# Reordering layer norms, value tiles and operand halves in a one-core gated cross-attention kernel

## The reference

```
x = x + tanh(g_xattn[0]) * L0_xattn(layernorm(x), ctx)        # 16 heads x 64, keys/values from 77 context tokens
x = x + tanh(g_ffn[0])   * L0_ffn(layernorm(x))               # ternary weights, int8-like activations, silu(gate)*up
x = x + tanh(g_xattn[1]) * L1_xattn(layernorm(x), ctx)
x = x + tanh(g_ffn[1])   * L1_ffn(layernorm(x))               # one expert's gelu ffn times its router probability

def L1_xattn(xx, ee):
    x = ln(xx, ln1)
    x = x + mha(x, x, a1, causal=True)      # 16 heads x 32, 512 keys; softmax over all keys, then the causal mask
    x = ln(x, ln2)
    return x + mha(x, ee, a2, causal=False) # keys and values from the 77 context tokens
# mha: xn = ln(x, lnx); yn = ln(y, lny); q, k, v; softmax(q k / sqrt(d)); o @ li1 + b + x;
#      then x_out + gelu(ln3(x_out) @ li2 + b) @ li3 + b
```

## Time and profile before

| | |
|---|---|
| median of 3 runs | 386.19 us (384.49 to 387.12) |
| the profiled execution | 386.85 us, span 385.1 us |
| mean granted TensorE clock in it | 0.972 |
| busy | PE 330.1 (86% of the span), DVE 285.7, ACT 271.5, POOL 122.7 us |

### The profile page before, as it was taken

The page is one execution under the profiler, slowest core; times in us unless marked ns, Lnnn a source line. Parts: engine busy times, 40 slices in busy tenths (PEclk is TensorE's granted clock), DMA queues, the critical chain, the costliest instruction groups (busy, mean ns, idle before and its releaser), DMA issues.

```text
span 385.1 us, 6932 instructions
## 1 busy us (share of the span) xinstructions
PE 330.1 (86%) x2165; PEld 233.5 (61%) x2165; DVE 285.7 (74%) x736; ACT 271.5 (70%) x957; POOL 122.7 (32%) x227
## 2 busy tenths in 40 slices
PE   5989999717698888898999889899896999978993
PEld 4868887503334554555646555576674888765673
DVE  0767779597886995979979889855586887846515
ACT  2378897847364998989999899914248888754441
POOL 1317665236512332223233233311023533421200
PEclk9999999968898999999999999999998999999999
DMA  6900000000019869403970896000000000000001
GB/s 197 361 9 1 2 3 0 0 1 3 0 43 211 184 143 211 84 2 69 212 159 1 178 212 214 3 2 0 2 2 1 1 2 0 3 0 2 0 2 54
DMA packets 6908, 24.75 MB, mean 64 GB/s; under 512 B 1451, under 2 KB 1528, under 8 KB 6136
## 3 DMA queue, kind: packets, MB, share of 16 engines
q1 hardware_dynamic: 6872, 24.31, 26.3%
HBM read 7.00 MB, written 0.52 MB: 20 GB/s over the span
## 4 chain that ended last, share of the span: by engine, by line
PE 45%; DVE 23%; ACT 16%; DMA 5%; issue 5%; SPq 3%; POOL 1%; DVEq 0%; ACTq 0%
PE ps L444 7%; PE ps L568 7%; PE ps L546 7%; ACT pring L1247 6%; PE ps L626 5%; PE ps L608 5%; DVE nm L1647 4%; PE ps L475 3%; SPq L884 3%; ACT arena L1121 3%; PE ps L496 3%; DMA stack<-sides 3%; PE ps L702 2%; ACT arena L1231 2%; PE ps L738 2%
## 5 line engine op out<-in xcount | busy, mean ns | idle before, releaser
L1647 DVE TENSOR_REDUCE nm<-ps 128x1 f32<-128x512 f32 x128 | 81.2, 678 | 17.0 <-PE ps L702 17.0
L1247 ACT ACTIVATE pring<-ps,nm 128x512 f32<-128x512 f32 x128 | 89.0, 725 | 6.4 <-DVE nm L1647 6.4
L1121 ACT ACTIVATE arena<-ps,nmx 128x77 f32<-128x77 f32 x256 | 79.2, 344 | 14.4 <-DVE nmx L1417 14.1
L1009 POOL TENSOR_SCALAR_AFFINE_SELECT pring<-pring 128x128 f32<-128x128 f32 x128 | 37.4, 295 | 80.9 <-ACT pring L1247 80.9
L702 PE MATMUL ps<-stack 128*128 128x512 f32 x128 | 55.2, 491 | 5.8 <-ACT pring L1247 2.4
L1121 ACT ACTIVATION_READ_ACCUMULATOR arena<-ps,nmx 128x1 f32 x256 | 57.2, 223 | 0.0
L974 POOL TENSOR_TENSOR arena<-arena,rden 128x616 f32<-128x616 f32 x32 | 39.2, 1226 | 51.3 <-DVE rden L1426 51.3
L444 PE MATMUL ps<-ident,pring 128*128 128x128 f32 x320 | 46.9, 275 | 5.9 <-ACT arena L1231 4.3
L444 PEld LDWEIGHTS ps<-ident,pring 128*128 128x128 f32 x320 | 36.5, 140 | 19.8 <-POOL pring L1009 10.7
L568 PEld LDWEIGHTS ps<-arena 128*128 128x128 f32 x320 | 38.9, 191 | 13.1 <-DVE arena L1433 11.7
L568 PE MATMUL ps<-arena 128*128 128x128 f32 x320 | 42.5, 280 | 4.9 <-DVE arena L1433 4.9
(11 more groups left out here) (149 smaller groups left out, 525.9 us busy)
## 6 DMA issues: line engine op xcount, KB each, us to landing
stack<-sides SPq DMA_DIRECT2D x32, 256.0 KB, 5.0
stack<-arena SPq DMA_DIRECT2D x16, 256.0 KB, 5.1
stack<-hid SPq DMA_DIRECT2D x12, 256.0 KB, 5.0
wa_sb<-in_wa SPq DMA_DIRECT2D x1, 1536.0 KB, 14.1
early<-in_w SPq DMA_DIRECT2D x2, 512.0 KB, 8.0
stack<-hid SPq DMA_DIRECT2D x8, 128.0 KB, 2.5
arena<-in_wa SPq DMA_DIRECT2D x1, 1024.0 KB, 4.8
pring<-in_wf SPq DMA_DIRECT2D x1, 768.0 KB, 10.7
```

The costliest lines, as they stand in the source:

```text
L1009: pool.affine_select(out=blk, in_=blk, compare_op=ALU.is_gt, fill=0.0, base=0, pattern=[[1, P]], channel_multiplier=-1).then_inc(masked, 1)
L1121: ins = act.activation(Pc[:, i % PC_SLOTS, h * HS:h * HS + M], bank(where[key])[:, h % 4 * HS:h % 4 * HS + M], ACT.Exp, bias=nmx[:, i % 4, ...
L1247: release(act.activation(pring[:, n % 2, i, :], bank(f"S{i}"), ACT.Exp, bias=nm1[:, n % 8, i:i + 1], accum_out=den1[:, n % 8, i:i + 1]), ( ...
L1647: dve.tensor_reduce(nm1[:, n % 8, i:i + 1], bank(f"S{i}"), AX.X, ALU.max, negate=True).then_inc(nm1_ready, 1)
```

## The change

1. Lead-in of the causal attention. VectorE does `low_half` 0 to 3 and the copies of value tiles 1 and 3 first and only then `ln1_gain(1)` and `ln1_bias(1)`. TensorE makes all four value tiles of batch 0 before the first scores (banks T0, T1, S1, S3) instead of two before and two in n = 0; the unread matmuls behind them are six into S0 instead of ten into S3. ScalarE copies tile 2 before the loop.
2. Causal attention, n = 5 and 6 on ScalarE. The "k" evacuation of batch 1 moves from n = 6 (between the exponentials) to the end of n = 5, and `sums_across(0)` from the end of n = 5 to n = 6, between the exponentials.
3. Second cross attention. `ln2_gain(1)` moves ahead of the units; `ln2_bias(1)` from i = 2, 3 to i = 0, 1; `ln_stats("a2", 1)` from i = 4 to two halves in i = 2 and 3; `ln_norm("a2", 1)` from i = 5 to two halves in i = 4 and 5; GpSimd's `power` from j = 3 to j = 2. The two additions of `a2_li1_b` move from i = 7, 8 to i = 10, 11. TensorE gets unread matmuls into bank A, five at i = 1 and two at i = 2.
4. Tails of both cross attentions. `ln_stats` of "a2f" and "f0", batch 0, from i = 13 to two halves in i = 13 and 14; `ln_norm` from i = 14 to 15; `power` from j = 12 to 13. `scale_x(0)` stays in i = 15, now behind `ln_norm`. The third ternary matrix is written at i = 17 instead of 13; `gate_up(0)` waits for two matrices and the first down product for the third.

```diff
-            def keep_busy(count):
-
+            def keep_busy(count, res="S3"):
+
+                pe.wait_ge(*last[res])
                 for _ in range(count):
-                    pe.matmul(bank("S3"), identb[:, :], wf0b[:, 0, :], start=True, stop=True)
+                    pe.matmul(bank(res), identb[:, :], wf0b[:, 0, :], start=True, stop=True)
...
+                    if site == "a2" and i in (1, 2):
+                        keep_busy(5 if i == 1 else 2, "A")
...
                         xq_transposes(0)
-                        pe.wait_ge(wq_ready, 3)
+                        pe.wait_ge(wq_ready, 2)
                         gate_up(0)
...
                     if t == 0:
+                        pe.wait_ge(wq_ready, 3)
                         claim(pe, res, ("out", "f0", b), filled_by=(f0_done, j + NT))
...
-            for t in range(2):
-                project_values(t, f"T{t % 2}")
-            keep_busy(10)
+            for t, res in enumerate(("T0", "T1", "S1", "S3")):
+                project_values(t, res)
+            keep_busy(6, "S0")
...
-                if n == 0:
-                    project_values(2, "T0")
                 if n < NHB:
                     scores(n, 2)
                     scores(n, 3)
-                if n == 0:
-                    project_values(3, "T1")
...
-                    if site == "l0" and j == 12:
+                    if site == "l0" and j == 13:
                         power("f0", batches=[0])
-                    if site == "a2" and j == 3:
+                    if site == "a2" and j == 2:
                         power("a2", batches=[1])
-                    if site == "a2" and j == 12:
+                    if site == "a2" and j == 13:
                         power("a2f", batches=[0])
...
             copy_values(0)
+            copy_values(2)
...
-                    if u == 0 and n in (5, 6):
-                        a1_evac(1, "qk"[n - 5])
-                if n == 0:
-                    copy_values(2)
-                if n >= HG and n % HG == 1:
+                    if u == 0 and n == 5:
+                        a1_evac(1, "q")
+                    if u == 0 and n == 6:
+                        sums_across(0)
+                if n == 5:
+                    a1_evac(1, "k")
+                if n > HG + 1 and n % HG == 1:
                     sums_across(n // HG - 1)
...
-                    if site == "a2" and i == 13:
-                        ln_stats("a2f", 0, xo)
-                    if site == "a2" and i == 14:
+                    if site == "a2" and i in (13, 14):
+                        ln_stats("a2f", 0, xo, range(2 * i - 26, 2 * i - 24))
+                    if site == "a2" and i == 15:
                         ln_norm("a2f", 0, xo)
...
-                    if site == "l0" and i == 13:
-                        ln_stats("f0", 0, r)
-                    if site == "l0" and i == 14:
+                    if site == "l0" and i in (13, 14):
+                        ln_stats("f0", 0, r, range(2 * i - 26, 2 * i - 24))
+                    if site == "l0" and i == 15:
                         ln_norm("f0", 0, r)
-                    if site == "l0" and i == 15:
                         scale_x(0)
                     if site == "a2" and i in (0, 1):
-                        ln2_gain(1, range(2 * i, 2 * i + 2))
+                        ln2_bias(1, range(2 * i, 2 * i + 2))
                     if site == "a2" and i in (2, 3):
-                        ln2_bias(1, range(2 * i - 4, 2 * i - 2))
-                    if site == "a2" and i == 4:
-                        ln_stats("a2", 1, x1)
-                    if site == "a2" and i == 5:
-                        ln_norm("a2", 1, x1)
-                    if site == "a2" and i in (7, 8):
-                        did(dve.tensor_tensor(xb[:, i - 7, :, :], x1[:, i - 7, :, :], row4("a2_li1_b"), ALU.add))
+                        ln_stats("a2", 1, x1, range(2 * i - 4, 2 * i - 2))
+                    if site == "a2" and i in (4, 5):
+                        ln_norm("a2", 1, x1, tiles=range(2 * i - 8, 2 * i - 6))
+                    if site == "a2" and i in (10, 11):
+                        did(dve.tensor_tensor(xb[:, i - 10, :, :], x1[:, i - 10, :, :], row4("a2_li1_b"), ALU.add))
...
-                    if site == "l0" and i in (9, 11, 13):
-                        ternary_bf16(i // 2 - 4)
+                    if site == "l0" and i in (9, 11, 17):
+                        ternary_bf16((9, 11, 17).index(i))
...
-            ln1_gain(1)
-            low_half(0)
-            ln1_bias(1)
-            for m in range(1, 4):
+            for m in range(4):
                 low_half(m)
             copy_values(1)
+            copy_values(3)
+            ln1_gain(1)
+            ln1_bias(1)
...
                 if n == 0:
-                    copy_values(3)
                     ln_stats("a1", 1, x1)
...
             ln_stats("ln2", 1, xo)
+            ln2_gain(1)
             cross("a2")
```

More of the change, by code:

```diff
@@ L668, in _ @@
                 if n == NB * NT:
-                    pe.wait_ge(*last["S3"])
                     keep_busy(6)
@@ L1307, in settle, with ln_stats @@
                     dve.wait_ge(*freed.pop(0))
-            def ln_stats(site, b, src):
-                for t in range(NT):
+            def ln_stats(site, b, src, tiles=range(NT)):
+                for t in tiles:
                     did(dve.bn_stats(stats[:, b, t, :], src[:, b, t, :]))
                 settle()
-                for t in range(NT):
+                for t in tiles:
                     did(dve.bn_aggr(mv[:, b, t, :], stats[:, b, t, :]))
+                if tiles[-1] < NT - 1:
+                    return
                 settle()
@@ L1320, in ln_stats, with ln_norm @@
                     .then_inc(var_ready, 1)
-            def ln_norm(site, b, src, affine=None, dst=None):
+            def ln_norm(site, b, src, affine=None, dst=None, tiles=range(NT)):
                 dve.wait_ge(rstd_ready, nth(site, b))
                 if affine is None:
-                    for t in range(NT):
+                    for t in tiles:
                         ins = dve.tensor_scalar(xn[:, b, t, :], src[:, b, t, :], mv[:, b, t, 0:1],
                                                 rstd[:, b, t:t + 1], ALU.subtract, ALU.mult)
+                    if tiles[-1] < NT - 1:
+                        did(ins)
+                        return
+                    settle()
                 else:
```

## The result

The changed kernel took 384.99 us (median of 20 executions, 382.45 to 386.07) against 387.63 (median of 20, 384.49 to 388.84) for the kernel before: ratio 0.9926, 95% interval 0.9905 to 0.9947. That is 2.64 us in the medians, 0.7%, faster than before and less than forecast. The median of before shown ahead of the prediction, 386.19, was of three of these executions.

A forecast was written before the change was run, and what follows sets the result against it. No engine was taken to bound the whole; TensorE, busiest, works 86% of the span. 2.05 - 0.65 + 2.0 + 1.1 + 0.35 = 4.85 us off 386.85 gave 382.0, or 381.4 against the 386.19 median; own range 380.2 to 382.6, wider 379.6 to 384.6.

The forecast's parts named there:

- lead-in (c): Causal attention's lead-in: head 1's first maxima follow head 0's without a gap, 2.05 us gained, bounds 0.5 to 2.6.
- exchange (d, e): Causal attention, n = 5 and 6: value product waits for the sums, delaying projection 8 and head 7's scores, 0.65 us lost.
- units of the second attention (f): Second cross attention: full clock held by unread matmuls, norm in halves, unit 8's scores earlier; 2.0 us gained, bounds 0.7 to 2.4.
- second tail (g, h): Second cross attention's tail: half the stats leave i = 13, unit 15's maxima start earlier; 1.1 us gained, bounds 0.6 to 1.3.
- first tail (a): First cross attention's tail: the same, but `scale_x` waits behind the norm; 0.35 us gained, bounds 0 to 0.7.
- fourth rival: At n = 6 TensorE idles 1.6 us and falls to half clock, costing at most 1.75 us: 383.1, chance 0.10.
- third rival: Lead-in bound by stacks: head 2's stack slips 1 to 1.5 us, reordering gives 0.8 us: 382.7, chance 0.12.

The follow-up runs named there:

- e10: The kernel before, no edit, one more single profiled execution: 384.90 us.
- e11: The kernel before, no edit, another single profiled execution: 386.37 us.
- e14: The kernel before, no edit, a single profiled execution to catch a long one: 386.32 us.
- e15: The kernel before, no edit, another single profiled execution to catch a long one: 388.20 us.
- e8: The changed kernel measured and profiled again, no edit: 385.64 us, ratio 0.9945; its profiled execution took 382.55 us.
- e12: The changed kernel, no edit, a single profiled execution: 383.94 us.
- e16: The changed kernel, no edit, a single profiled execution to catch a long one: 383.00 us.
- e18: The changed kernel, no edit, a single profiled execution to catch a long one: 384.80 us.
- e17: The changed kernel, no edit, a single profiled execution: 385.05 us.
- e4: The changed kernel with the exchange undone (k evacuation back in head 6, sums back at the end of head 5): 382.24 us, ratio 0.9891.
- e5: The changed kernel plus six unread matmuls into bank B at n = 6, ahead of the waiting value product: 382.89 us, ratio 0.9883.
- e6: The kernel before with 18 instead of 10 unread matmuls ahead of the causal attention's first scores: 385.41 us, ratio 0.9961.
- e2: The kernel before with only the second cross attention's changes, including its seven unread matmuls: 385.19 us, ratio 0.997.
- e1: The kernel before with only the lead-in changes (halves, four value tiles, copies, six unread matmuls): 384.73 us, ratio 0.9959.
- e13: The kernel before, nothing reordered, with 18 instead of 10 lead-in unread matmuls and seven in the second cross attention: 384.97 us, ratio 0.9955.
- e9: The changed kernel with the sums, then the k evacuation directly behind them, at the end of head 5: 382.76 us, ratio 0.9889.

## Why the prediction was wrong

The mechanisms of the sum were all seen; most of its terms were mis-sized, and one choice between rivals was wrong. In the means over the profiled executions (five of before: this study's first, e10, e11, e14, e15; six of the changed kernel: the first, e8, e12, e16 to e18):

| | forecast | pair of first profiles | means |
|---|---|---|---|
| lead-in (c) | +2.05 | +2.22 | 5.43 - 3.80 = +1.63 |
| exchange (d, e) | -0.65 | -0.85 | 25.67 + 142.35 - 27.14 - 142.79 = -1.91 |
| units of the second attention (f) | +2.0 | +1.84 | 24.50 - 21.89 = +2.61 |
| second tail (g, h) | +1.1 | +0.68 | +0.68 |
| first tail (a) | +0.35 | 0.0 | 0.0 |
| ternary ffn and rest of the lead-in (b) | 0 | -0.37 | 41.91 - 42.24 = -0.33 |
| sum | 4.85 | 3.5, with 0.83 at the start 4.35 | 2.68 |

2.68 us is near what the medians moved by (2.64), and in part by luck. With the first maxima, which come 0.21 earlier in the mean, the profiles differ by 2.89, the means of the twenty executions by 2.94. But the profiled executions are on both sides 0.8 us shorter than the twenty, and among the changed kernel's they hold too few with the stretch behind n = 6, so the price of the exchange here is more likely too low than too high.

**The step that failed** is the exchange. I forecast 0.65 us of bare wait and nothing for the clock behind it; the wait measured 0.85, and that was right in kind, but the whole exchange cost 1.91 in the means. In the fourth rival I had the rest: TensorE idling 1.6 us at n = 6 and a stretch at half clock behind it, for at most 1.75 us more, chance 0.10. It idles 1.69 us, and of the six profiled executions three (e12, e17, e18) have the stretch and pay 1.6 to 2.6 us above the bare wait; the other three don't. e4 and e5 show the cause: take the added idling away, or fill it, and no execution is above 383.01, where 24 of the changed kernel's 30 (the twenty and e8) lie above 383.5. An event that falls in half of the executions or more belonged into the forecast, with its price times its chance, since the row beside it (1.90 us of idling, then 0.50) said so; 0.10 was far too low.

**Part 1** was mis-sized the same way from the other side. The 2.05 us are right against the profiled execution, and every step of it held: low halves, tiles at 114.2 (110.17 + 3.60, here 0.5 us earlier in all), norm in front of the first maxima, no gap to head 1 (3.81 us against 3.80 forecast). But of the gaps that I removed, and had put down to the value tiles between the scores, 1.5 us were TensorE at half clock, which e10 and e14 of before don't have: there the old order takes 4.51 us and the new one gains 0.7. I took a stretch of one execution for the kernel's. The same stretch was what the unread matmuls of e6 remove without any reordering. The stack of head 2 (third rival) comes late in some: TensorE waits for it 1.43 to 1.50 us in e2, e10 and e14, and VectorE, which has work, doesn't. In e1 it waits 2.60 us, and head 7 comes 0.83 us later. In the changed kernel's six profiles the 1.36 to 1.43 us of idling in that place end with ScalarE's exponential, which frees the bank, and cost nothing.

**Part 3** held: bias beside GpSimd 1.54 us (1.53 forecast), unread matmuls that push nothing and hold the clock in every profile that has them, scores gapless from unit 3, unit 8 at 21.89 us where 21.73 (23.73 - 2.0) was forecast. Against the mean of the profiles it gives more than forecast, since before's stretch lasts twice as long in two of five (25.45 and 25.60 us). In the two units the norm halves took 0.82 and 0.63 us; the first met GpSimd's product, which I had expected it to miss. The Trainium skill (GPSIMD Engine Reference, Specifications) names contention of the two engines at the SBUF for VectorE's instructions with two SBUF inputs; 1.54 us for the bias pair, which has them, agrees in kind.

**Part 4.** In the second tail unit 15's maxima came 0.99 us nearer (1.07 forecast), but 0.31 was lost behind them: TensorE's value product of unit 13 waits 0.83 us for copies that wait for its own transposes, and this loop, not ScalarE, sets when unit 14's transposes go. In the first tail the norm in front of `scale_x` took all: the rounding waits 1.11 us for the scale. I had put `scale_x` at 1.1 us behind a norm that ends at 68.5; counted from the same start it was 1.24 behind 68.7, and 0.35 us was too fine a remainder to forecast.

**The level.** 381.4 stood on 386.19, a median of three; twenty give 387.63. Even so 4.85 us was too much by 2.2. The loss of 0.33 us in (b) is explained only in part: it is there in all profiles of the changed kernel (42.12 to 42.31 against 41.87 to 41.93), also with the tails alone (42.27) and with only unread matmuls in other places (42.12), so no part has it alone. Some 0.2 us of it goes with where the first half-clock stretch of the ffn lies: in the changed kernel (b) is 42.12 where it begins near 79 us (e8, e17) and 42.30 where near 81 to 82 (the other four), and up to head 0 e6 and e13 are the same program, with 41.91 at 78 and 42.12 at 81. The rest stays open. Which part of an idle place decides whether the clock falls in a given execution was not tried either.

**The best version** measured is the changed kernel with part 2 undone (e4, 0.9891) or with both pieces at the end of head 5 (e9, 0.9889) or with the idling filled (e5, 0.9883); among the three the measurement doesn't choose. e4 and e5 also scatter least (0.8 and 0.6 us in six executions each; e9 2.4 in six, the changed kernel 3.6 in twenty). The exchange undone and its 1.09 us filled as well was not tried.

## What to carry to other kernels

Where TensorE idles a microsecond or more in the middle of its work, ask not only what the wait costs but what the clock does behind it, in several executions: one profile shows one draw. Compare kernels by distances between landmarks and look at the list of execution times before trusting a pair of profiles; groups of times some 1.5 to 2 us apart were stretches at half clock here. A few unread matmuls in such a gap can be worth more than a reordering, and before an exchange of two pieces on a full engine, ask which of the two the in-order reader needs first.

## What the runs showed of the hardware

TensorE's clock makes most of the scatter, the start up to 0.9 us of it. With the kernel unchanged, TensorE idling 1.90 us was followed by 0.50 at 117 to 121 in three of five executions and not in two; idling of 1.35 and 0.44 us in the second cross attention by 0.50 in all five, for about 3.5 us in three and about 7 in two; idling of 0.75 and 1.69 us at n = 6 in three of six, in one of them (e17) before the idling had ended. Idling of 1.09 us in the same place was followed by none in the five of before, but by one in e2 and one in e13; idling of 1.33 us at the end of the second cross attention and of 1.36 to 1.55 us ahead of head 2 by none in any profile, idling of 2.60 us there (e1) by a short stretch. So the length of one gap alone does not tell. A short stretch cost 1.5 to 1.6 us in the lead-in and at n = 6, 0.74 in the second cross attention (22.64 - 21.89) and nothing at the kernel's end; a long one cost up to 2.6, TensorE working all the time and VectorE and ScalarE waiting for it (windows of e17). The Trainium skill (TensorE: Matmul & The Clock Gate, What's actually happening) says that at the start of a kernel's matmuls the place where the gate changes differs from run to run of the same kernel. The traces agree: the same 31 matmuls near the start take 3.83 to 4.60 us in the kernel before. And they show the same inside the kernel, where it comes to groups of executions 1.5 to 4 us apart.

Filling such a place with unread matmuls, each 0.23 us long, held the clock in all three places tried: ahead of the first stack (e6, e13), at n = 6 (e5) and in the second cross attention (e2, e13 and every profile of the changed kernel). It cost nothing where the wait outlasts them.
